# Where a transformer kernel computes its conditioning layers: 16 or 14 of them ahead of the dense halves, and caps on GpSimd or on ScalarE

## What is computed

```python
decay = exp(-exp(w)) * (0.5 + 0.5 * tf)                 # per sequence and channel
ek    = exp(min(side, 30)); ekv = ek * side             # key = value = side
nf, df = scan(ekv), scan(ek)                            # a = a * decay + in, along the sequence
nb, db = the same scans backward
euk   = exp(min(u + side, 30))
num, den = nf + nb - ekv + euk * side, df + db - ek + euk
cond  = sigmoid(r) * num / max(den, 1e-8) * (0.8 + 0.2 * tf)
x = x + (cond0(x) @ weight.T * scale + bias)            # level 0, r = x
x = x + moe(cond1(x))                                   # level 1: r is the x of the line above
```

## Time and profile before

| | us |
|---|---|
| runs, median of 3 | 4742.23 (4740.93 to 4744.61) |
| the profiled execution's own time | 4735.88 |
| its span, first to last instruction | 4734.2 |
| TensorE busy | 4476.6 (95%) |
| VectorE busy | 2502.9 (53%) |
| ScalarE busy | 1794.9 (38%) |
| GpSimd busy | 834.6 (18%) |
| mean granted TensorE clock | 0.973 |

### The profile page before, as it was taken

The page is one execution under the profiler, slowest core; times in us unless marked ns, Lnnn a source line. Parts: engine busy times, 40 slices in busy tenths (PEclk is TensorE's granted clock), DMA queues, the critical chain, the costliest instruction groups (busy, mean ns, idle before and its releaser), DMA issues.

```text
span 4734.2 us, 60632 instructions
## 1 busy us (share of the span) xinstructions
PE 4476.6 (95%) x19926; PEld 3553.3 (75%) x19927; DVE 2502.9 (53%) x2708; ACT 1794.9 (38%) x2597; POOL 834.6 (18%) x992
## 2 busy tenths in 40 slices
PE   6778999999999946999999999999999999999999
PEld 2346787777778734778888888888888888888887
DVE  8999999999998411433143333444432143233432
ACT  6655555555554301232132323333331142222331
POOL 4410100101000062111111111111211111111211
PEclk9988999999999967999999999999999999999999
DMA  6777888988888624564254453655643345444443
GB/s 254 271 239 233 278 293 270 302 269 289 280 253 301 208 79 137 201 248 111 58 168 107 122 161 89 221 159 153 202 132 89 62 142 186 115 111 111 146 128 62
DMA packets 253977, 857.11 MB, mean 181 GB/s; under 512 B 28832, under 2 KB 61728, under 8 KB 229024
## 3 DMA queue, kind: packets, MB, share of 16 engines
q1 hardware_dynamic: 172944, 572.77, 34.1%
q0 software_dynamic: 53776, 182.09, 18.0%
q10 hardware_dynamic: 27136, 100.67, 5.6%
HBM read 652.40 MB, written 181.01 MB: 176 GB/s over the span
## 4 chain that ended last, share of the span: by engine, by line
PE 83%; issue 4%; DVE 3%; DMA 2%; ACT 0%; POOL 0%; POOLq 0%; DVEq 0%; ACTq 0%
PE ps L1822 33%; PE ps L1686 26%; PE ps L1836 16%; PE ps L1755 3%; PE ps L1708 1%; PE ps L1811 1%; PE ps L1696 1%; DMA work<-rows_dram,row_idx 1%; PE ps L1706 1%; PE ps L1722 1%; DVE halves L1558 0%; DVE work L1178 0%; DVE work L1195 0%; DVE work L1169 0%; DVE halves L1446 0%
## 5 line engine op out<-in xcount | busy, mean ns | idle before, releaser
L1822 PE MATMUL ps<-halves 128*128 128x512 f32 x7152 | 1695.5, 393 | 3.5 <-DVE halves L1563 2.8
L1686 PE MATMUL ps<-halves 128*128 128x512 f32 x6144 | 1469.6, 397 | 114.3 <-issue 106.2
L1822 PEld LDWEIGHTS ps<-halves 128*128 128x128 f32 x7152 | 1336.9, 189 | 278.4 <-DVE halves L1563 3.1
L1686 PEld LDWEIGHTS ps<-halves 128*128 128x128 f32 x6144 | 1159.2, 189 | 401.5 <-issue 159.0
L1836 PE MATMUL ps<-halves 128*128 128x512 f32 x3576 | 834.9, 389 | 1.3 <-DVE halves L1579 1.3
L1836 PEld LDWEIGHTS ps<-halves 128*128 128x128 f32 x3576 | 671.1, 188 | 140.9 <-DVE halves L1579 1.6
L1563 DVE TENSOR_TENSOR halves<-ps,halves 128x1024 fp32r<-128x1024 f32 x150 | 183.7, 1225 | 902.5 <-ACT halves L985 902.5
L594 POOL DMA_INDIRECT out<-work,add_idx x149 | 249.8, 1677 | 1420.4 <-DVE work L1585 1219.8
L1558 DVE TENSOR_TENSOR halves<-work,halves 128x1024 fp32r<-128x1024 f32 (+1 forms) x320 | 440.2, 1433 | 83.5 <-ACT halves L989 83.5
L985 ACT ACTIVATE halves<-ps 128x1024 fp32r<-128x1024 f32 x150 | 154.0, 1027 | 859.6 <-PE ps L1822 859.6
L989 ACT ACTIVATE halves<-work 128x1024 fp32r<-128x1024 f32 (+1 forms) x320 | 369.1, 1229 | 67.7 <-PE ps L1836 57.3
(11 more groups left out here) (222 smaller groups left out, 3798.7 us busy)
## 6 DMA issues: line engine op xcount, KB each, us to landing
halves<-split_dram SPq DMA_DIRECT2D x512, 512.0 KB
work<-expert_w SPq DMA_DIRECT2D x192, 1024.0 KB, 5.6
split_dram<-halves ACTq DMA_DIRECT2D x32, 1024.0 KB, 5.2
plain<-shared_w SPq DMA_DIRECT2D x32, 512.0 KB, 3.4
work<-side_t ACTq DMA_DIRECT2D x32, 512.0 KB, 6.7
gated_dram<-work ACTq DMA_DIRECT2D x32, 512.0 KB, 5.1
work<-x_t ACTq DMA_DIRECT2D x32, 512.0 KB, 5.7
ratio_dram<-second ACTq DMA_DIRECT2D x32, 512.0 KB, 5.1
```

The costliest lines, as they stand in the source:

```text
L1686: last = pe.matmul(bank(k % 4), w, op[:, part], start=(c == 0 and w is w_hi and op is hi), stop=(c == CB - 1 and w is w_lo))
L1822: last = pe.matmul(ps_h[:, a * 512:a * 512 + 512], xp[:, xk * P:(xk + 1) * P], wp[:, rhs], start=(xk == 0 and xp is xhi and wp is whi[q]), ...
```

## The change

- The second layers of the first two units of each group of four, from unit 4 on (4, 5, 8, 9, ... 28, 29), move one group later. A list JOBS gives the order of all 64 layers. 14 are ahead of half 0; each of halves 0 to 5 holds eight jobs of 4 fills: slots 0 and 1 the late second layers, 2 and 3 first layers alone, 4 to 7 two units whole; half 6 holds the last two in its fills 0 to 7.
- A late layer and a layer alone load `side` anew and compute `ek` again (`side_exp`, 6 per half instead of 4); these `single` jobs form the value product in place in EK behind the forward scan. A job that opens a side runs its first fill first, then h_edge.
- min(a, 30) becomes 30 - Relu(30 - a): ScalarE computes Relu(cap - side), then Exp(cap + u' - that), for `ek` everywhere and for the third term in the stage ahead. GpSimd's `clip` and `clip_alone` are gone.
- The 32 splits are given to the 14 jobs, three to each second layer of units 0 to 3, two to each other. x has a second buffer in the stage ahead and is loaded a unit earlier.
- Blocks 4 to 7 of the channels are permuted (UNIT_OF), the ratio loads of the last two blocks of a half stand at fills 8 and 11, ranks move to fills 12, 13, 14 and 17 of half 6.

```diff
@@ constants @@
+LATE = UNITS_PER_HALF // 2
+UNIT_OF = (0, 1, 2, 3, 6, 7, 4, 5)
+def has_late_layer(u):
+    return u >= UNITS_PER_HALF and u % UNITS_PER_HALF < LATE
+JOBS = [(u, l) for u in range(ALONE) for l in range(2) if not (l and has_late_layer(u))]
+JOBS_ALONE = len(JOBS)
+for first in range(ALONE, BLOCKS, UNITS_PER_HALF):
+    JOBS += [(first - UNITS_PER_HALF + q, 1) for q in range(LATE)]
+    JOBS += [(first + q, 0) for q in range(LATE)]
+    JOBS += [(first + q, l) for q in range(LATE, UNITS_PER_HALF) for l in range(2)]
+JOBS += [(BLOCKS - UNITS_PER_HALF + q, 1) for q in range(LATE)]
+SIDE_FIRST = [n for n, (u, l) in enumerate(JOBS) if l == 0 or has_late_layer(u)]
+for n in range(JOBS_ALONE):
+    SPLIT_AT.append(SPLIT_AT[-1] + (3 if n in (1, 3, 5, 7) else 2))
...
-    return STEP_L[o - 4] + 3 if o >= 4 else o // 2
+    return (STEP_L[0] + 3, STEP_L[1] + 3, STEP_L[5], STEP_L[7])[o - 4] if o >= 4 else o // 2
+RANK_AT = (12, 13, 14, 17)
@@ gpsimd @@
-            def clip(u, side):
...
-                pool.tensor_scalar(EK, side, 30.0, None, ALU.min).then_inc(s["kc"], 1)
...
-                pool.tensor_scalar(E_alone[l], side_alone[u % 2], side_cap[:, u + l * BLOCKS:u + l * BLOCKS + 1], None, ALU.min)\
@@ scalar @@
-            def side_exp(u):
-                sc.wait_ge(s["kc"], u + 1)
-                sc.activation(EK, EK, ACT.Exp).then_inc(s["ek"], 1)
+            def side_exp(i):
+                n = SIDE_FIRST[i]
+                sc.wait_ge(*side_landed(i))
+                if i and single(n - 1):
+                    sc.wait_ge(s["nf"], n)
+                elif i:
+                    sc.wait_ge(s["h_fwd"], n)
+                    sc.wait_ge(s["ekv"], i)
+                apart(sc)
+                sc.activation(EK, side_buffer(n), ACT.Relu, scale=-1.0, bias=thirty[:, 0:1]).then_inc(s["kc"], 1)
+                sc.wait_ge(s["kc"], i + 1)
+                sc.activation(EK, EK, ACT.Exp, scale=-1.0, bias=thirty[:, 0:1]).then_inc(s["ek"], 1)
@@ scalar, job(n, fill), in the halves @@
+                if opens_side:
+                    fill(0)
+                enter(n, F)
+                if prompt(n):
+                    enter_numerator(n)
+                third_exp()
+                if l == 0 and part != 4:
+                    sigmoid_x(u)
+                if opens_side or prompt(n):
+                    fill(1)
+                else:
+                    fill(0)
+                if not prompt(n):
+                    enter_numerator(n)
+                if pending(n):
+                    store_result(n - 1)
...
+                inverse()
...
+                fill(2)
+                if part == 4:
+                    sigmoid_x(u)
+                fill(3)
...
+                elif n + 1 in SIDE_FIRST:
+                    side_exp(SIDE_AT[n + 1])
@@ scalar, alone(n, fill) @@
+                for p in range(SPLIT_AT[n], SPLIT_AT[n + 1]):
+                    split_raw_hi(p)
...
+                enter(n, F)
+                enter_numerator(n)
...
+                sc.activation(E, side_buffer(n), ACT.Relu, scale=-1.0, bias=side_cap[:, at:at + 1]).then_inc(s["wc"], 1)
+                sc.wait_ge(s["wc"], n + 1)
+                sc.activation(E, E, ACT.Exp, scale=-1.0, bias=side_end[:, at:at + 1]).then_inc(s["euk"], 1)
+                if l == 0:
+                    sigmoid_x(u)
+                    fill(1)
                 else:
+                    fill(4)
+                    if u < ALONE - 1:
+                        side_exp(SIDE_AT[n + 1])
+                for p in range(SPLIT_AT[n], SPLIT_AT[n + 1]):
+                    split_raw_lo(p)
...
+                if l == 0 and has_late_layer(u):
+                    side_exp(SIDE_AT[n + 1])
@@ vector, job(n, fill), in the halves @@
+                def numerator_forward():
+                    if single(n):
+                        ve.wait_ge(s["h_fwd"], n + 1)
+                        ve.tensor_tensor(EK, EK, side, ALU.mult).then_inc(s["ekv"], 1)
+                    ve.wait_ge(s["ekv"], i + 1)
+                    if pending(n):
+                        ve.wait_ge(s["num_added"], added(n - 1))
+                    ve.tensor_tensor_scan(G, d, EK if single(n) else EKV, 0.0, ALU.mult, ALU.add).then_inc(s["nf"], 1)
+                if opens_side:
+                    fill(0)
+                    ve.wait_ge(s["ek"], i + 1)
+                    if not single(n):
+                        ve.tensor_tensor(EKV, EK, side, ALU.mult).then_inc(s["ekv"], 1)
+                ve.tensor_tensor_scan(F, d, EK, 0.0, ALU.mult, ALU.add).then_inc(s["h_fwd"], 1)
...
@@ tensor @@
-            for u in range(ALONE):
-                for l in range(2):
-                    split_raw(u, 2 * l)
-                    split_raw(u, 2 * l + 1)
-                    denominator(u, l)
-                    numerator(u, l)
+            for n in range(JOBS_ALONE):
+                for p in range(SPLIT_AT[n], SPLIT_AT[n + 1]):
+                    split_raw(p)
+                denominator(n)
+                numerator(n)
```

More of the change, by code:

```diff
@@ L489, in store_out, with job @@
                 sp.dma_start(to, RS_OF[o % 2].rearrange("p (t c) -> p t c", c=P)).then_inc(out_sem[o % 2], 16)
-            def unit(u, par, fill, prompt, pending):
-                for i in range(FILLS_PER_UNIT):
+            def job(n, fill):
+                for i in range(FILLS_PER_JOB):
                     fill(i)
@@ new lines, in enter, with enter_numerator @@
+            def enter(n, F):
+                u, l = JOBS[n]
+                at = u + l * BLOCKS
+                sc.wait_ge(s["h_fwd"], n + 1)
+                apart(sc)
+                sc.activation(edge_in[:, 0:1], F[:, SEQ - 1:SEQ], ACT.Copy, scale=edge[:, at:at + 1]).then_inc(s["h_edge"], 1)
+            def enter_numerator(n):
+                u, l = JOBS[n]
+                at = u + l * BLOCKS
+                sc.wait_ge(s["nf"], n + 1)
+                apart(sc)
+                sc.activation(edge_in[:, 1:2], G[:, SEQ - 1:SEQ], ACT.Copy, scale=edge[:, at:at + 1]).then_inc(s["n_edge"], 1)
@@ L728, in h_edge, with sigmoid_x, job, third_exp @@
+            def sigmoid_x(u):
+                sc.wait_ge(*x_landed(u))
+                sigmoid(x_buffer(u), x_buffer(u), "sig_steps", u, "sig_x")
+            def job(n, fill):
+                u, l = JOBS[n]
+                at, part = u + l * BLOCKS, slot(n)
+                opens_side = n in SIDE_FIRST
+                def third_exp():
+                    sc.wait_ge(*result_stored(n - 2))
                     apart(sc)
-                    sc.activation(edge_in[:, 0:1], F[:, SEQ - 1:SEQ], ACT.Copy, scale=edge[:, ds(u + l * BLOCKS, 1)])\
-                        .then_inc(s["h_edge"], 1)
@@ L756, in unit @@
-                h_edge(0)
-                if prompt:
-                    n_edge(0)
-                euk(0)
-                sc.wait_ge(s["x_in"], (u + 1) * 16)
-                sigmoid(x_of[par], x_of[par], "sig_steps", u, "sig_x")
-                fill(1)
-                if not prompt:
-                    n_edge(0)
-                if pending:
-                    store_ratio(u - 1)
-                inverse(0)
+                    sc.activation(N, F, ACT.Ln, bias=low[:, at:at + 1]).then_inc(s["g_ln"], 1)
@@ new lines, in inverse @@
+                    if part not in (3, 4, 6) and n + 2 < len(JOBS):
+                        sc.wait_ge(s["wv_done"], n + 1)
+                        if part == 0:
+                            load_side(n + 2)
+                        if part == 1:
+                            load_x(JOBS[n + 1][0])
+                            sc.wait_ge(s["nf"], n)
+                            load_side(n + 2)
+                        if part in (2, 5):
+                            load_x(JOBS[n + 1][0])
+                        if part == 7:
+                            load_side(n + 2)
@@ L1002, in _ @@
             sc.activation(neg_round, neg_ident, ACT.Copy).then_inc(s["neg_set"], 1)
-            with_halves(sc, alone, unit, fill, tail)
+            with_halves(sc, alone, job, fill, tail)
             def split_weights(j, q, g):
@@ L1565, in _ @@
             ve.wait_ge(s["masks"], 9)
-            with_halves(ve, alone, unit, fill, tail)
+            with_halves(ve, alone, job, fill, tail)
             def split_weights(j, q):
```

614 lines of the change are left out of this document (288 added, 326 removed).

## The result

The changed kernel takes 4777.18 us (median of 4 runs, 4772.60 to 4781.76), the kernel before, on the same chip, 4741.58 (4 runs, 4738.42 to 4744.61): the ratio is 1.0077, 95% interval 1.0064 to 1.0089, so it is slower by 35.6 us. Forecast were 4775 us and 0.71 for slower. The profiled execution took 4775.76 us, its span is 4774.1; against the profiled execution of before that is 39.9 us more.

What follows compares the result with a forecast made beforehand. VectorE was taken to bound the stage ahead and half 0's first part, TensorE dense halves 1 to 5 with VectorE close behind. -12 + 6.5 + 37 + 1.2 = +32.7 us on the 4742.23 median gave 4775 us, range 4728 to 4800.

Steps and rivals of the forecast that it cites:

- the stage ahead: Before the first dense half: 12 us shorter (-16 to -8, distant end -47), ScalarE's queue keeping it from VectorE's rate.
- signs of being right: Halves 1 to 5: root() 205 to 209 us apart, backward scan waiting behind a square; first dense product near 274 us.
- the two stalls of the third split: Second layers, units 0 to 3: edge stall 2.1 to 2.4 us; third term at 28.1 instead of 25.6 us.
- Rival 4: VectorE/GpSimd port: a full lock would give back 104 us, total 4683 us; chance 0.01.
- Half 0: First part of dense half 0, 292 to 375 us: +6.5 us, from border waits and added value products.
- Halves 1 to 5: Dense halves 1 to 5: 7.4 us longer each, 37 us together.
- the edge at fill 4: Slot 1: h_edge behind a square waiting for TensorE's sum; VectorE's backward scan 7.4 us late, with no idleness to recover.
- the borders: Between jobs in dense halves: VectorE waits for sigmoid (2.2 to 2.3 us) and exponential (0.9), 3.2 us at 11/12.
- The slowed clock: Dense halves: TensorE at half clock after idleness could raise a half's 7.4 us to 9; only in the range.
- Half 6: Last two late layers in fills 0 to 7, ranks moved to later fills: +1.2 us.
- Rival 1: Dense halves: lateness at fill 4 absorbed, stage ahead gains 20 to 47 us; total 4703 to 4730 us; chance 0.16.
- mark of being wrong: Either root() distances of 200 us in the dense halves, or a stage ahead that ends before 265 us.

Runs made afterwards that it cites:

- e4: Kernel before with only the caps moved from GpSimd to ScalarE as positive parts: 4739.7 us, ratio 1.0003.
- e6: Changed kernel, stage ahead only: in second layers third high split behind third term's exponential, key's exponential behind low splits: 4769.5 us, ratio 1.0063.
- e1: Changed kernel with ScalarE's square of block 1 at step 5 instead of 4: 4763.8 us, ratio 1.0050.
- e3: Changed kernel with block 1's square a step later, and at job borders the cap and exponential a step earlier and forward scan ahead of the opening step: 4749.2 us.
- e5: Changed kernel with slots 1 and 3 in the old second-layer order on both engines, their cap and exponential one step earlier: 4734.1 us, ratio 0.9988.
- e12: Changed kernel with slots 1 and 3 in the old order, but every job's cap and exponential left at the end of the job before: 4785.8 us, ratio 1.0103.
- e10: Changed kernel with the old order in slot 3 alone, and that slot's cap and exponential one step earlier: 4761.5 us, ratio 1.0047.
- e8: Changed kernel without the Relu, the caps at 30 of key and third term left out: 4746.4 us, ratio 1.0015.

## Why the prediction was right, and where it was not

The direction came out, and the size nearly. Part of that is luck: the stage ahead gained 10.2 us more than forecast, and halves 1 to 6 lost 8.4 us more, so that two errors of opposite sign left +30.8 for +32.7. Of the signs of being right, all five halves had the edge wait behind a square, and three of the five took 205 to 209 us; the other two took 212.

**The stage ahead: right in kind, 10 us short.** Units 0 to 3 cost +9.8 us. The lower of the two sums in the forecast was 10.8 (its own 2.3 us a unit gives 9.2; no other term is named); it took 15 for a slow clock. The clock did fall, four matmuls of the first split took 3.44 us where 1.98 is usual, but TensorE was idle another 1.40 us before the third split, which waits for ScalarE (L884), so it lengthened nothing. Units 4 and 5 gave -24.0 (forecast -23.4), unit 6 -5.3 (-5.2). Unit 7, forecast at +1.0, gave -2.0, and the opening -0.6 where +0.6 stood. The unit lengths were right: 34.5 us (34.8) and 20.4 (20.8). e4 confirms the caps' terms by themselves, and e6 the two stalls of the third split, of which the order of issue explains a little less than half.

**The port.** The long scans went with GpSimd's caps, and no more than they: 1.8 us a unit in e4, 0.7 of the 2.4 lost to ScalarE's stall. By the Trainium skill (SBUF — State Buffer, "SBUF: two separate sides") the loser of the shared pair blocks for the whole instruction. The trace doesn't agree: caps of 4.5 us lengthened an operation by 0.8. Rival 4 is out.

**Half 0: right**, +6.5 us, with the waits at the places and of the sizes given (the terms as they are listed add up to 6.85).

**Halves 1 to 5: the sum was right within a sixth (37 for 43.6), its attribution was not.** The step that failed is the one of dense halves 1 to 5: all 7.4 us of a half were derived from the edge at fill 4, with the later slots carrying lateness on. Measured, the edge alone is 14.8 us of the 43.6 (e1). The forecast had counted the borders (3.2 and 2.2 us) but let them stand as links of the same chain, and said that the lateness reaches TensorE at root()'s z. In half 3 it reaches TensorE before that: by a read-out of VectorE, late from the half before (3.31 us of idleness at 879 us), by a square (2.44), and by the copy at step 15 behind slot 3's inverse (2.00); at z only 0.70 are left. "On the way TensorE loses some of it earlier, at a sum and at a transpose, which changes nothing" was the wrong sentence: e3 took away nearly all waits for edge and borders and kept 206 us, and only the order of the layer against the steps, with the exponential a step earlier (e5), brought the halves back. The slowed clock, held for an end of the range, goes with 18.2 of the 43.6 us: in e5, at a granted clock of 1.00, the same matmuls are busy 990.7 us, here 1008.4 at 0.98. The Trainium skill (TensorE: Matmul & The Clock Gate, Part 1) has the array at half clock after idleness. The trace agrees in kind: the stretches around idle times of 2 to 3.3 us show granted clocks of 0.87 to 0.95.

**Half 6:** +3.0 for +1.2; not pursued, and open. It takes 200.5 us in e5 too, so the order in slots 1 and 3 is not its cause.

**The rivals.** Rival 1 named as its sign a backward scan in slot 1 less than about 2 us behind the forward scan: from the end of the one to the start of the other it was 1.7 us in half 2 and 5.1 in half 3, and the halves took 207.4 and 212.0 us. The sign was there in part and the rival false: in half 2 TensorE still waited for a square and for the copy of step 15. One mark of being wrong was a stage ahead that ends before 265 us, and by the first dense product it was met: that is at 264.7 us, where 274 was forecast. The stage gained more than was thought, and the time came out nevertheless.

## What to carry to other kernels

When work is cut into pieces that each open like the first, the order that the old second piece had (scan before step, edge before square) was doing something: look at what stands behind each wait for another engine, and try that order before blaming the added work. Putting a scan ahead of a step needs its operand ready a step earlier, and either edit alone can be worth nothing or less (e12). Where two engines run within a few per cent of each other, removing one lateness can only uncover the next: with slot 3 mended alone, TensorE waited at the same place for another engine (e10). And a forecast whose sum comes out has not had its mechanism tested: here an experiment on the named cause gave back a third.

## What the runs showed that was not expected

- A matmul stream pays for short idle times twice: in half 3, 3.31 us of idleness were followed by 144 matmuls in 34.56 us, where the half before had them in 32.92 after 0.57 us. Not every wait does it: in the kernel before they took 32.95 us behind 2.13 us. Over halves 1 to 5 the slower matmuls were 18.2 us beside 25.4 of more idleness. The windows around the wait of 3.31 us and those of 2.44 and 2.00 us show the clock (columns as above):

```profile
879.99:893.23 13.24, 10.63 (x40) 8.65 (x41) 8.11 (x9) 5.86 (x8) 0.00 (x0) 0.87 0.84 278
...
959.47:972.72 13.25, 10.81 (x46) 8.07 (x44) 10.13 (x10) 11.66 (x15) 0.00 (x0) 0.95 0.99 370
972.72:985.97 13.25, 11.25 (x45) 8.24 (x45) 13.11 (x12) 8.00 (x11) 0.85 (x1) 0.92 0.75 235
```

- The unchanged last 2835 us of the program vary by 10 us between the kernels' profiles (2830.7 to 2840.6), 0.2% of the whole, and halves 1 to 5 by 6 us with the same code (e6); a comparison of two profiled spans has to be made up to a mark ahead of it.
- ScalarE's Relus, 34 us of busy time over halves 1 to 5 (623.2 for 589.1 in e8), cost nothing that shows in the dense halves (1.9 us) and some 20 us in the stage ahead, where its queue sets the pace.
